# Two blocks' scatters at a time, directly ahead of norm1: a change to the order of GpSimd's queue in the first attention

## The chip, the cores and the metric

The kernel runs on one core of one Trainium2 chip. The metric is the time of one execution on the device in microseconds (us), lower is better. Engines: TensorE (PE, with its weight loads PEld), VectorE (DVE), ScalarE (ACT), GpSimd (POOL) and SyncE (SP), each with its own queue of instructions.

## What is computed

Two layers on x of 32 blocks of 128 tokens with 256 features. Each layer adds an attention and then a mixture of experts, both on a layer-normalised x:

```python
x = x + L0_xattn(layernorm(x), ctx, itok, mask, ...)   # 16 heads, masked by equal layer indices
x = x + L0_ffn(layernorm(x), router, w1, w2, scale)    # 8 experts, top 2, silu
x = x + L1_xattn(layernorm(x), ctx, ...)               # both directions, gated
x = x + L1_ffn(layernorm(x), ...)                      # 8 experts, top 2, capacity 640
```

In L0_ffn each token goes to its two best experts. The kernel therefore makes, for each block of 128 tokens, two lists of 128 slots (k = 0 and 1), and writes the tokens' numbers at those slots into a table in DRAM.

## The kernel before, in words

The program has four stages one after the other: first attention (a_*), first experts (b_*), second attention (c_*), second experts (d_*). In each stage every engine has a function that writes its whole queue out by hand. Engines meet by semaphores only.

**First attention.** A software pipeline over blocks b. In iteration b of its loop (b from 0 to NB + 4 = 36) GpSimd does work for different blocks: norm2(b - 2), the last three small steps of the second layer norm's factors (lines 449 to 453, behind VectorE's statistics of line 922); mask(b + 1) (line 465); add_bias(b - 1) (line 471); norm1(b + 4), the same for the first layer norm (lines 437 to 441, behind line 906). ScalarE reads norm1's result in L531 and norm2's in L625. VectorE works out the slots of a group of blocks at once (slots_out, lines 1012 to 1026); the groups are six of four blocks (0 to 23) and four of two (24 to 31). Its slots_out of a group whose last block is l runs in VectorE's iteration l + 4 and raises slot_ready.

**Scatters.** GpSimd writes each block's 128 token numbers to DRAM with two indirect DMAs (line 479, k = 0 and 1), 64 in all. The table `turn` says in which iteration a block's turn comes: for groups of four in iteration first + 8 + j, one block each iteration; for blocks 24 to 31, two blocks each in iterations 33, 34, 35 and 36. In an iteration with a turn the k = 0 scatters stand between mask and add_bias, and the k = 1 scatters behind norm1.

**The seam to the first experts.** After its loop GpSimd waits until all scatters have landed (line 511). Then b_pool waits for t_ready, which VectorE raises with etab (line 1230) at the end of `tables`, which in turn follows the last slots_out. Then come load_ids (line 1163: row numbers from the scattered table) and gather (line 1171: the rows). ScalarE and VectorE split the rows in two parts (lines 1275 and 1253), SyncE transposes them by DMA, and TensorE starts the first expert block (line 1324).

Of the kernel before, what the change touches and what calls it, by code (L numbers as in the profile page):

```python
# [23 lines left out]
NB = 32  # L24
# [33 lines left out]
def build(nc, a, out):  # L58
    with ExitStack() as ctx:
# [22 lines left out]
        def sem(name):  # L82

            s = nc.alloc_semaphore(name=name)
            owned.append(s)
            return s
# [4 lines left out]
        def dram_ids(name, n, k):  # L91
            return nc.dram_tensor("dram_" + name, (n, k), I32, kind="Internal").ap()
# [6 lines left out]
        ids = [dram_ids("ids0", SPARE0 + P, 1), dram_ids("ids1", SPARE1, 2)]  # L99
# [45 lines left out]
        tokens = sb("tokens", [P, NB], I32)  # L145
# [26 lines left out]
        def due(v):  # L172

            return not isinstance(v, int) or v > 0
# [32 lines left out]
        scat = [sem(f"a_scat{i}") for i in range(4)]  # L207
# [3 lines left out]
        def first_attention():  # L211
# [3 lines left out]
            def sa(name, shape, dt=F32):  # L215
                return work(name, shape, dt)
# [42 lines left out]
            RG = 4  # L259
# [5 lines left out]
            gslot, gsidx = sa("gslot", [P, RG * 2]), sa("gsidx", [P, 4, RG * 2], U32)  # L265
# [28 lines left out]
            cnt_done, cnt_read, slot_steps, slot_ready = (psem(n) for n in ("cnt_done", "cnt_read", "slot_steps", "slot_ready"))  # L294
# [3 lines left out]
            GROUPS = [(b, RG) for b in range(0, NB - 2 * RG, RG)] + [(b, 2) for b in range(NB - 2 * RG, NB, 2)]  # L298
            group_of = {}
# [4 lines left out]
            def inside(b):  # L304
                return 0 <= b < NB

            def last_of(b):

                if not inside(b):
                    return None  # L310
                g, j, n = group_of[b]
                return g if j == n - 1 else None
# [88 lines left out]
            def a_pool(pool):  # L401
                bound = pool.to_reg(SPARE0 - 1)
# [28 lines left out]
                def norm1(b):  # L431
                    if inside(b):
                        p = b % 2
                        pool.wait_ge(n1_stat, b + 1)
                        if due(b - 1):
                            pool.wait_ge(xn_ready, b - 1)
                        pool.tensor_scalar(rstd1[:, p, 0:1], mv1[:, p, 1:2], EPS, None, ALU.add).then_inc(n1_rstd, 1)
                        pool.wait_ge(n1_rstd, b * 3 + 1)
                        pool.tensor_tensor(rstd1[:, p, 0:1], rstd1[:, p, 0:1], minus_half[:, :], ALU.pow).then_inc(n1_rstd, 1)
                        pool.wait_ge(n1_rstd, b * 3 + 2)  # L440
                        pool.tensor_scalar(rstd1[:, p, 1:2], mv1[:, p, 0:1], rstd1[:, p, 0:1], -1.0, ALU.mult, ALU.mult).then_inc(n1_rstd, 1)
# [25 lines left out]
                def add_bias(b):  # L467

                    if inside(b):
                        pool.wait_ge(xn_ready, b + 1)  # L470
                        pool.tensor_tensor(x8[:, b % 8, :], x8[:, b % 8, :], bob[:, :], ALU.add).then_inc(res_ready, 1)

                def scatter(b, k):

                    g, j, n = group_of[b]
                    if j == 0 and k == 0:
                        pool.wait_ge(slot_ready, g + 1)
                    at = 2 * j + k
                    pool.indirect_dma_start(ids[0], bass.IndirectOffsetOnAxis(ap=gsidx[:, g % 4, at:at + 1], axis=0),  # L479
                                            tokens[:, b:b + 1], None, bounds_check=bound, oob_is_err=False).then_inc(scat[g % 4], 16)  # L480


                turn = {}
                for g, (first, n) in enumerate(GROUPS):
                    for j in range(n):
                        b = first + j
                        turn.setdefault(first + n + 4 + j if n == RG else NB + 4 - (NB - 1 - b) // 2, []).append(b)

                norm1(0)
                mask(0)  # L490
# [6 lines left out]
                norm1(3)  # L497
                pool.wait_ge(bo_ready, 1)
                pool.wait_ge(s_const, 64)
                for b in range(NB + 5):  # L500
                    norm2(b - 2)
                    if b > 0:
                        mask(b + 1)
                    for c in turn.get(b, ()):
                        scatter(c, 0)
                    add_bias(b - 1)
                    norm1(b + 4)
                    for c in turn.get(b, ()):
                        scatter(c, 1)
                for p in range(4):  # L510
                    pool.wait_ge(scat[p], scattered(len(GROUPS) - 1, p))

# [598 lines left out]

            a_sems = owned[kept:]
            return a_sync, a_pool, a_act, a_pe, a_dve, clear


# [1387 lines left out]
```

## Time and profile before

| | |
|---|---|
| median of three runs | 1536.67 us (1535.08 to 1537.13) |
| the profiled execution | 1535.08 us, span 1533.3 us |
| busy: TensorE, weight loads | 1355.9 us (88%), 1100.8 us (72%) |
| busy: VectorE, ScalarE, GpSimd | 848.4, 815.3, 669.3 us |
| first attention | up to about 391 us |
| first expert matmul | 429.28 us |
| the 64 scatters of line 479 | 68.2 us busy |

The profile is of one execution. The span runs from the first to the last recorded instruction, and the execution's own time is 1.8 us longer. Busy time is that of an engine's instructions; semaphore waits and the issue of DMAs by SyncE aren't counted in it. "Issue" in the chain of waits is time in which the engine waited for nothing that the profile shows.

### The profile page before, as it was taken

How to read it: one execution, taken by the hardware profiler on the slowest of the kernel's cores; microseconds unless marked ns; L12 is line 12 of the kernel's file. 1: busy time of each engine (PE TensorE's matmuls, PEld its weight loads, DVE VectorE, ACT ScalarE, POOL GpSimd, SP SyncE). 2: the span in 40 equal slices, each digit the busy share in tenths (PEclk: the TensorE clock that was granted, in tenths of full speed). 3: DMA queues.
4: the chain of work that ended last, by engine and by line, in shares of the span. 5: the costliest groups of instructions: out<-in, count | busy, mean ns of one | idle time of the engine just before them, and what ended most of it. 6: DMA issues, size and time to landing. Idle time of an engine off the chain costs nothing.

```text
span 1533.3 us, 37441 instructions
## 1 busy us (share of the span) xinstructions
PE 1355.9 (88%) x12922; PEld 1100.8 (72%) x12922; DVE 848.4 (55%) x2343; ACT 815.3 (53%) x1904; POOL 669.3 (44%) x935
## 2 busy tenths in 40 slices
PE   5999999997159999999997899999992899999996
PEld 4787777775126666667665788888881799999995
DVE  4787787876512323232222577777763566666663
ACT  3787777775035555554553555555551445545452
POOL 3234545453563333332301456666656344444422
PEclk8999999998579999999999999999995999999998
DMA  4333434341049999988886222232213343443331
GB/s 113 111 113 98 120 94 106 104 90 53 11 87 183 187 204 184 179 170 145 166 170 138 65 84 83 84 84 83 84 54 74 94 131 109 130 127 108 121 114 51
DMA packets 280856, 172.76 MB, mean 113 GB/s; under 512 B 212990, under 2 KB 259424, under 8 KB 280676
## 3 DMA queue, kind: packets, MB, share of 16 engines
q1 hardware_dynamic: 257940, 134.65, 38.3%
q0 software_dynamic: 18608, 32.14, 7.7%
q10 hardware_dynamic: 4128, 3.57, 0.8%
q8 instruction: 112, 1.84, 0.6%
q14 instruction: 68, 0.56, 0.2%
HBM read 93.40 MB, written 31.80 MB: 82 GB/s over the span
## 4 chain that ended last, share of the span: by engine, by line
PE 77%; DVE 5%; issue 4%; ACT 4%; DMA 3%; POOL 3%; another core or an unknown queue 1%; SPq 1%; ACTq 0%; DVEq 0%; POOLq 0%
PE psum L2267 14%; PE psum L1337 11%; PE psum L1324 11%; PE psum L2280 7%; PE psum L1804 3%; PE psum L1885 3%; PE psum L1810 3%; PE psum L797 2%; PE psum L726 2%; PE psum L700 2%; PE psum L739 2%; PE psum L814 2%; PE psum L800 2%; PE psum L1875 2%; PE psum L778 2%
## 5 line engine op out<-in xcount | busy, mean ns | idle before, releaser
L1260 DVE SCALAR_TENSOR_TENSOR b_h<-b_hid,b_h 128x1024 f16<-128x1024 f32 x71 | 87.0, 1226 | 283.8 <-ACT b_h L1289 278.7
L2267 PE MATMUL psum<-d_xT,d_w 128*128 128x256 f16 (+1 forms) x2304 | 230.0, 256 | 3.8 <-DVE d_xT L2356 2.9
L1324 PE MATMUL psum<-arena,b_xT 128*128 x852 | 200.0, 386 | 32.6 <-DMA b_xT<-b_x 32.1
L2267 PEld LDWEIGHTS psum<-d_xT,d_w 128*128 128x128 f16 x2304 | 199.6, 98 | 24.5 <-issue 2.5
L1337 PE MATMUL psum<-arena,b_hT 128*128 x1704 | 200.9, 274 | 14.1 <-issue 7.4
L1337 PEld LDWEIGHTS psum<-arena,b_hT 128*128 128x128 f16 x1704 | 166.4, 98 | 52.7 <-issue 19.4
L1324 PEld LDWEIGHTS psum<-arena,b_xT 128*128 128x128 f16 x852 | 84.6, 99 | 123.6 <-issue 40.7
L1284 ACT ACTIVATE b_hid<-psum 128x512 f32<-128x512 f32 x142 | 84.6, 597 | 137.1 <-PE psum L1324 83.9
L1171 POOL DMA_INDIRECT b_xg<-dram_normed,b_gi x71 | 67.3, 948 | 206.8 <-DVE b_x L1253 195.1
L2321 ACT ACTIVATE d_sg<-psum 128x256 f32<-128x256 f32 (+1 forms) x192 | 65.9, 348 | 143.9 <-PE psum L2267 135.9
L2366 DVE SCALAR_TENSOR_TENSOR d_hf<-psum,d_sg 128x256 f32<-128x256 f32 (+1 forms) x192 | 71.2, 379 | 103.7 <-ACT d_sg L2321 86.8
L2280 PE MATMUL psum<-d_w,d_h 128*128 128x256 f16 x960 | 115.5, 273 | 0.7 <-DVE d_h L2371 0.7
L594 ACT ACTIVATE pT<-psum,amc 128x512 f32<-128x512 f32 x128 | 77.5, 688 | 47.1 <-PE psum L726 47.1
L2280 PEld LDWEIGHTS psum<-d_w,d_h 128*128 128x128 f16 x960 | 90.9, 98 | 11.0 <-DVE d_h L2371 1.0
L1621 POOL DMA_INDIRECT c_yg<-dram_expert_rows,c_gi x64 | 64.8, 1012 | 70.2 <-DMA dram_expert_rows<-b_ys 55.2
L941 DVE TENSOR_REDUCE mx<-psum 128x4 f32<-128x512 f32 x128 | 79.5, 683 | 25.6 <-PE psum L700 25.4
L2229 POOL DMA_INDIRECT out<-d_rowsum,d_gi x40 | 42.1, 1053 | 92.4 <-DVE d_rowsum L2381 85.1
L2224 POOL DMA_INDIRECT d_rowsum<-out,d_gi x40 | 43.2, 1079 | 87.5 <-PE psum L2267 63.1
L1163 POOL DMA_INDIRECT b_gi<-dram_ids,ypos x71 | 67.4, 950 | 27.2 <-issue 27.2
L1289 ACT ACTIVATE b_h<-b_hid 128x1024 f16<-128x1024 f32 x71 | 75.0, 1057 | 4.6 <-DMA b_hT<-b_h 2.5
L1656 POOL DMA_INDIRECT dram_ids<-c_gsidw,c_gsidx x64 | 67.6, 1057 | 19.4 <-issue 19.4
L479 POOL DMA_INDIRECT dram_ids<-tokens,gsidx x64 | 68.2, 1066 | 12.9 <-issue 12.9
(319 smaller groups left out, 2933.0 us busy)
## 6 DMA issues: line engine op xcount, KB each, us to landing
d_wst<-in_L_w SPq DMA_DIRECT2D x64, 384.0 KB
stage<-in_L_w SPq DMA_DIRECT2D x32, 512.0 KB
dram_expert_rows<-b_ys SPq DMA_DIRECT2D x71, 128.0 KB
ctxT<-in_ctxT SPq DMA_DIRECT2D x64, 128.0 KB
dram_normed<-xn SPq DMA_DIRECT2D x64, 128.0 KB
x<-in_x SPq DMA_DIRECT2D x32, 128.0 KB, 4.9
dram_x<-xnew SPq DMA_DIRECT2D x32, 128.0 KB
c_x<-dram_x SPq DMA_DIRECT2D x32, 128.0 KB
```

The lines of the kernel that those rows point to most:

```text
L479: pool.indirect_dma_start(ids[0], bass.IndirectOffsetOnAxis(ap=gsidx[:, g % 4, at:at + 1], axis=0), tokens[:, b:b + 1], None, bounds_check ...
L594: act.activation(pT[:, r, :, :].rearrange("p j q -> p (j q)"), psum[:, SB + r, :], ACT.Exp, bias=amc[:, b:b + 1]).then_inc(exp_done[r], 1)
L941: i = dve.tensor_reduce(mx[:, r, :], psum[:, SB + r, :].rearrange("p (j k) -> p j k", j=HB), AX.X, ALU.max)
L1260: dve.scalar_tensor_tensor(out=h16[:, p, 1, :], in0=hid[:, p, :], scalar=H_SCALE, in1=h16[:, p, 0, :], op0=ALU.mult, op1=ALU.subtract).the ...
L1284: act.activation(hid[:, p, half * 512:(half + 1) * 512], psum[:, 1 + 2 * p + half, :], ACT.Silu, scale=1.0 / (X_SCALE * W_SCALE)).then_inc ...
L1289: act.activation(h16[:, p, 0, :], hid[:, p, :], ACT.Copy, scale=H_SCALE).then_inc(hi_done, 1)
L1324: i = pe.matmul(psum[:, 1 + 2 * p + half, :], xT[:, j % NT, px, c, :], weights(e, c, pw, half * 512, 512), start=(n == 0), stop=(n == len( ...
L1337: i = pe.matmul(psum[:, 6 + p, 0:D], hT[:, p, ph_, c, :], weights(e, 2 + c // 4, pw, (c % 4) * D, D), start=(n == 0), stop=(n == len(terms ...
L1656: pool.indirect_dma_start(ids[1], bass.IndirectOffsetOnAxis(ap=gsidx[:, g % 3, at:at + 1], axis=0), gsidw[:, g % 3, at, :], None, bounds_c ...
L2267: i = pe.matmul(psum[:, q, m * n:(m + 1) * n], w16[:, fc % RING, pw, col:col + P], xT[:, p, px, c, at:at + n], start=(k == 0), stop=(k == ...
L2280: i = pe.matmul(psum[:, NQ + k, 0:D], h16[:, fc % 2, ph_, k * P:(k + 1) * P], w16[:, fc % RING, pw, 2 * DC * P:UW], start=(fc == 0 and t = ...
L2366: dve.scalar_tensor_tensor(out=hf[:, fc % 2, at:at + n], in0=psum[:, q, n:2 * n], scalar=H_SCALE / (X_SCALE * W_SCALE), in1=sg[:, fc % 2, ...
```

## The change

The table `turn` is gone. scatter(b) now issues both indirect DMAs of a block, one behind the other, and the loop calls it in one place only, between add_bias and norm1. When the group of block b - 5 ends with that block, the group's first two blocks are scattered in iteration b; when the group of block b - 6 ends with that block, its third and fourth are. For a group whose last block is l these are iterations l + 5 and l + 6. Blocks 24 to 31 thus have their turns in iterations 30, 32, 34 and 36. Nothing else is changed.

```diff
--- before.py
+++ after.py
@@ -470,21 +470,15 @@
                         pool.wait_ge(xn_ready, b + 1)
                         pool.tensor_tensor(x8[:, b % 8, :], x8[:, b % 8, :], bob[:, :], ALU.add).then_inc(res_ready, 1)
 
-                def scatter(b, k):
-
-                    g, j, n = group_of[b]
-                    if j == 0 and k == 0:
-                        pool.wait_ge(slot_ready, g + 1)
-                    at = 2 * j + k
-                    pool.indirect_dma_start(ids[0], bass.IndirectOffsetOnAxis(ap=gsidx[:, g % 4, at:at + 1], axis=0),
-                                            tokens[:, b:b + 1], None, bounds_check=bound, oob_is_err=False).then_inc(scat[g % 4], 16)
-
-
-                turn = {}
-                for g, (first, n) in enumerate(GROUPS):
-                    for j in range(n):
-                        b = first + j
-                        turn.setdefault(first + n + 4 + j if n == RG else NB + 4 - (NB - 1 - b) // 2, []).append(b)
+                def scatter(b):
+                    if inside(b):
+                        g, j, n = group_of[b]
+                        if j == 0:
+                            pool.wait_ge(slot_ready, g + 1)
+                        for k in range(2):
+                            at = 2 * j + k
+                            pool.indirect_dma_start(ids[0], bass.IndirectOffsetOnAxis(ap=gsidx[:, g % 4, at:at + 1], axis=0),
+                                                    tokens[:, b:b + 1], None, bounds_check=bound, oob_is_err=False).then_inc(scat[g % 4], 16)
 
                 norm1(0)
                 mask(0)
@@ -497,16 +491,18 @@
                 norm1(3)
                 pool.wait_ge(bo_ready, 1)
                 pool.wait_ge(s_const, 64)
+
                 for b in range(NB + 5):
                     norm2(b - 2)
                     if b > 0:
                         mask(b + 1)
-                    for c in turn.get(b, ()):
-                        scatter(c, 0)
                     add_bias(b - 1)
+                    for last, at in ((b - 5, 0), (b - 6, 2)):
+                        if last_of(last) is not None:
+                            first, n = GROUPS[last_of(last)]
+                            for j in range(at, min(at + 2, n)):
+                                scatter(first + j)
                     norm1(b + 4)
-                    for c in turn.get(b, ()):
-                        scatter(c, 1)
                 for p in range(4):
                     pool.wait_ge(scat[p], scattered(len(GROUPS) - 1, p))
```

## Rows read from the trace of the kernel before

**Rows 1.** Windows: us; each engine's busy (x instructions); PEclk, DMA share, GB/s.
```profile
286.35:330.14 43.79, 41.60 (x597) 33.40 (x593) 34.56 (x105) 33.77 (x84) 22.98 (x41) 1.00 0.40 103
...
391.37:418.54 27.17, 1.98 (x10) 1.40 (x10) 16.64 (x71) 1.49 (x5) 16.57 (x18) 0.50 0.03 5
...
480.00:840.00 360.00, 351.68 (x2427) 239.17 (x2425) 100.97 (x132) 188.97 (x322) 104.76 (x114) 1.00 0.92 173
```

**Rows 2.** Waits from 154 to 330: us in total, times, longest us.
```profile
POOL rstd L437 <- DVE mv L906: 68.7, 16, 6.0
```

**Rows 3.** The chain of waits in the seam: start us, us, what.
```profile
406.24 8.14 DMA dram_ids<-tokens,gsidx
414.38 4.16 issue
```

**Rows 4.** GpSimd's timeline in the seam: start us, us, engine, line, operation, [idle before].
```profile
391.11 0.26 POOL L453 TENSOR_SCALAR rstd<-mv,rstd 128x1 f32<-128x1 f32 x1
391.54 1.07 POOL L479 DMA_INDIRECT dram_ids<-tokens,gsidx  x1 [0.16 <-issue]
392.92 0.98 POOL L479 DMA_INDIRECT dram_ids<-tokens,gsidx  x1 [0.30 <-issue]
...
411.69 0.97 POOL L479 DMA_INDIRECT dram_ids<-tokens,gsidx  x1 [0.30 <-issue]
418.54 1.00 POOL L1163 DMA_INDIRECT b_gi<-dram_ids,ypos  x1 [5.87 <-issue]
```

**Rows 5.** VectorE's timeline in the seam.
```profile
392.38 0.21 DVE L1026 CAST gsidx<-gslot 128x4 uint32<-128x4 f32 x1
...
398.26 0.16 DVE L1026 CAST gsidx<-gslot 128x4 uint32<-128x4 f32 x1
...
407.28 0.20 DVE L1230 CAST etab<-b_tables 128x71 int32<-128x71 f32 x1
```

**Rows 6.** The chain of waits at the second attention's end.
```profile
1174.46 2.07 DMA dram_ids<-c_gsidw,c_gsidx
```

**Rows 7.** Timeline of GpSimd, ScalarE and VectorE, one iteration of the steady part.
```profile
286.35 0.24 POOL L437 TENSOR_SCALAR rstd<-mv 128x1 f32<-128x1 f32 x1 [5.63 <-DVE mv L906]
...
287.34 0.27 POOL L441 TENSOR_SCALAR rstd<-mv,rstd 128x1 f32<-128x1 f32 x1
287.77 1.08 POOL L479 DMA_INDIRECT dram_ids<-tokens,gsidx  x1 [0.16 <-issue]
...
288.93 0.23 POOL L449 TENSOR_SCALAR rstd<-mv 128x1 f32<-128x1 f32 x1
...
290.14 0.74 POOL L465 TENSOR_SCALAR other<-tokr,tokc 128x128 f32<-128x128 f32 x1
291.06 1.08 POOL L479 DMA_INDIRECT dram_ids<-tokens,gsidx  x1 [0.18 <-issue]
292.18 0.73 POOL L471 TENSOR_TENSOR x<-x,bob 128x256 f32<-128x256 f32 x1
...
295.86 0.62 ACT L531 ACTIVATE xn<-x,rstd 128x256 f32<-128x256 f32 x1
296.24 0.18 DVE L906 BATCH_NORM_AGGREGATE mv<-st 128x2 f32<-128x6 f32 x1
296.35 0.62 ACT L625 ACTIVATE xn<-xnew,rstd 128x256 f32<-128x256 f32 x1
```

**Rows 8.** GpSimd's timeline in the drain, iterations 32 and 33.
```profile
380.90 0.23 POOL L449 TENSOR_SCALAR rstd<-mv 128x1 f32<-128x1 f32 x1 [7.16 <-DVE mv L922]
...
382.10 0.72 POOL L471 TENSOR_TENSOR x<-x,bob 128x256 f32<-128x256 f32 x1
390.14 0.22 POOL L449 TENSOR_SCALAR rstd<-mv 128x1 f32<-128x1 f32 x1 [7.32 <-DVE mv L922]
```

**Rows 9.** Timeline of TensorE and ScalarE at the start of the experts.
```profile
429.28 10.22 PE L1324 MATMUL psum<-arena,b_xT 128*128 x36 [32.07 <-DMA b_xT<-b_x]
...
444.11 0.60 ACT L1284 ACTIVATE b_hid<-psum 128x512 f32<-128x512 f32 x1 [7.75 <-remote]
```

**Rows 10.** Line 479 alone: duration ns min/median/max, first and last start us.
```profile
L479 POOL DMA_INDIRECT dram_ids<-tokens,gsidx x64: 971/1078/1525, 114.7 to 411.7; - x64
```

## The prediction

> **What bounds the kernel now.** I read the table of windows first. While blocks flow steadily, four blocks take 43.79 us and TensorE is busy for 41.60 of them at the full granted clock (1.00, 2.4 GHz); GpSimd is busy for 22.98 [rows 1]. So TensorE with its short hand-overs sets the pace there, and GpSimd has spare time. The list of waits of that stretch says the same from the other side: GpSimd waits for VectorE (68.7 us in 16 waits, 4.3 us each, before norm1), and among the waits of the other engines none names GpSimd as the one waited for [rows 2]. From 391.37 to 418.54 the picture turns over: 27.17 us in which TensorE is busy for 1.98, VectorE for 16.64 and GpSimd for 16.57 [rows 1]. This is the seam between the first attention and the first experts.
>
> In the seam the chain of waits runs through GpSimd alone: scatter after scatter of L479, then a transfer of 8.14 us and 4.16 us charged to nothing, until the first row-number load of the experts at 418.54 [rows 3]. GpSimd's timeline shows the whole row of them: 16 of the 64 scatters start from 391.54 to 411.69, all of them after the last norm2 [rows 4]. They are the scatters of blocks 24 to 31, which the old table of turns puts in iterations 33 to 36, while norm2 of block 31 is in iteration 33. The reader is to see that these 20 us are a backlog and not work waiting for its input. VectorE hands over the slots of the last but one pair at 392.38 + 0.21 = 392.59 and of the last pair at 398.26 + 0.16 = 398.42, and the last table that the experts' first load needs (etab) at 407.28 + 0.20 = 407.48 [rows 5]. GpSimd is behind all three.
>
> **The change, part by part.** (1) *What moves out of the seam.* With the new rule, blocks 24 and 25 scatter in iteration 30, 26 and 27 in iteration 32, 28 and 29 in 34, 30 and 31 in 36. Of the 16 scatters in the seam, 8 leave it. The number of scatters stays 64, and the wait for slot_ready stays one for each group.
>
> (2) *The new seam.* It starts as before, at 391.37, with the end of norm2 of block 31 (391.11 + 0.26). Blocks 28 and 29 wait for slots until 392.59. The first scatter of the old run starts 0.16 us after the engine is free, the second starts 392.92 − 391.54 = 1.38 us later, and from the second to the last are 14 steps in 18.77 us, with two long ones among them; I take the common step, 0.97 us of work and 0.30 us of gap, 1.27 [rows 4]. So the four start at 392.75, 394.13, 395.40 and 396.67 and GpSimd is free at 397.9. The last four wait for slots until 398.42 and start at 398.58, 399.96, 401.23 and 402.50. The last scatter thus starts 411.69 − 402.50 = 9.19 us earlier.
>
> (3) *From the last scatter to the experts' first load.* GpSimd waits until every scatter has landed. Before, the load starts 418.54 − 411.69 = 6.85 us after the last scatter's start [rows 4]. How much of this is landing and how much depends on the backlog isn't shown. From below: in the same place of the second attention the chain gives a scatter's landing as 2.07 us [rows 6]; then the last one would be down at 404.57, the tables at 407.48 would decide, and with 0.30 of gap the load starts at 407.78, a gain of 10.76. From above: the chain gives 8.14 us for the fifth from the end [rows 3]; with the same gap the load starts at 402.50 + 8.14 + 0.30 = 410.94, a gain of 7.60. I take 6.85, since it is measured on the same scatter with the same three ahead of it at the same spacing: the load starts at 409.35 and the gain is 9.19. The tables (407.48) are then 1.9 us early.
>
> The Trainium skill ("DMA: Bandwidth & Descriptors", Anatomy of one DMA — SWDGE (gpsimd) path) gives such a transfer a fixed cost of about 2.0 us beside its bytes, most of it the wait for the write's receipt. By it the tables would decide and the estimate would be a gain of 10.8. The row of the second attention agrees with it (2.07), the row of this seam doesn't (6.85, if all of it is landing).
>
> (4) *The steady part: 12 bursts of four in place of pairs, the last two of them in the drain.* For groups of four, iterations 0 and 1 modulo 4 get four scatters each after add_bias and the other two get none. In the old iteration, norm1 runs from 286.35 to 287.61, a scatter lies ahead of norm2 (287.77) and another behind mask (291.06), and add_bias ends at 292.91. Without the two, norm2, mask and add_bias close up: 1.24 us are saved ahead of norm2 and 1.26 behind mask, so add_bias ends at 290.41. The burst starts 0.17 later and takes 1.08 + 3 × 1.27 = 4.89, until 295.47. The next norm1 can't start before its statistics, 296.24 + 0.18 = 296.42 [rows 7]. The cover is GpSimd's wait for VectorE, and 0.95 us of it are left. If that cover is gone, norm1 is late, and what is late next is the normalisation on ScalarE, L531: it starts at 295.86 for a norm1 that ended at 287.61, 8.25 us of further slack [rows 7]. Price: nothing. norm2 gets earlier by 1.2 us, and its reader on ScalarE (L625) starts at 296.35 anyway [rows 7], so there is no gain either.
>
> (5) *The drain.* Here iterations wait for norm2's statistics and bursts lie in those waits. The tightest is the last, blocks 26 and 27 in iteration 32: norm2 of block 30 starts at 380.90 and add_bias ends at 382.10 + 0.72 = 382.82; the burst ends at 382.82 + 0.17 + 4.89 = 387.88, and the norm2 of block 31 starts at 390.14 [rows 8]. 2.26 us are left. Without that cover each us would be lost one for one, as ScalarE, the logits and the last slots hang on this norm2. Price: nothing.
>
> (6) *Behind the seam.* The first expert matmul starts at 429.28 after 32.07 us without TensorE work [rows 9]; it moves with the load, 10.74 us behind it. From 480 to 840 TensorE is busy for 351.68 of 360.00 us [rows 1], so the experts are bound by work of fixed length and the gain is carried to the end. What isn't sure is the start of the experts: ScalarE waits 7.75 us for something that the trace doesn't name, until 444.11 [rows 9]. I take it as unchanged, with 3 us either way for the range. The granted clock is 0.50 (1.2 GHz) all through the seam, after TensorE had nearly stopped [rows 1], and still when the experts start; I expect the same.
>
> **The sum.** −9.19 (seam) + 0 (steady) + 0 (drain) = −9.2. The profiled execution has a span of 1533.3 and took 1535.08, so it would become 1524.1 and 1525.9. The median of the three runs is 1536.67, 1.6 above that execution; from it I get 1527.5 us, 0.60% less. A measurement of this kernel can tell about 0.2% (3.1 us) from no change.
>
> **The rivals.** (a) *The landing is short and the tables decide.* For it: 2.07 us in the second attention [rows 6]. Against it: the scatters there hold another record and may drop more rows, and here 6.85 us passed. Time: 1536.67 − 10.76 = 1525.9. Chance 0.15. (b) *Given back at the experts' start*, by the unnamed waits or a clock that rises later: half of the gain is lost. For it: the 7.75 us wait; against it: all that feeds it moves along. Time: 1532.1, chance 0.10. (c) *No change*: the experts' first load is held by something else that stands at 418. For it: 4.16 us of the chain before that load are charged to nothing [rows 3]. Against it: 6.85 us is short for another cause to hide behind. Time: 1536.7, chance 0.05. (d) *Slower: bursts of four stall GpSimd in the steady part.* Place: between add_bias and norm1, iterations 8 to 29. It decides once a burst exceeds 4.89 + 0.95 + 8.25 = 14.09 us, 3.5 us for a scatter; from there each us costs 12. With 4.0 us a scatter it is (16.0 − 14.09) × 12 = 23 us, less the 9 of the seam: 1550.5. Against it: the longest of 64 scatters takes 1.525 us, the 16 in a row included [rows 10]. Chance 0.03.
>
> **How the numbers follow.** The forecast has 0.67 and gives 1527.5; its own range is 7.60 to 10.76 of gain and 3 us of the start, 1523 to 1532. (a) lies inside, (b) at its edge. I give 1524.0 to 1532.5, which leaves out (c), (d) and little of the rest. Faster by over 0.2% is the forecast, (a) and most of (b): 0.90. Within 0.2%: (c) and the rest of (b): 0.07. Slower: 0.03.
>
> **What the changed profile would show.** Right: 8 scatters between norm2 of block 31 and the experts' first load, in two runs of four with a gap of about 0.7 us before the second; the load at 409.4 (407.8 would mean the tables, 410.9 a longer landing); the first expert matmul at 420.1; TensorE's idle time before it near 23 us. The four-block period stays at 43.8 us and GpSimd's idle time before norm1 falls to about 1 us after bursts and grows after the others. Wrong: norm1 or norm2 of the steady part named as a wait of ScalarE; norm2 of block 31 later than 390.2; a scatter of over 2 us; or a gap between the load and the first matmul of more than 11 us.

## The result, and the profile of the changed kernel

The change makes the kernel slower.

| | before | changed |
|---|---|---|
| median of four runs, same chip | 1535.88 us (1533.14 to 1537.13) | 1556.24 us (1552.75 to 1562.42) |
| ratio | | 1.014, 95% interval 1.0104 to 1.0175 |
| profiled execution, its span | 1535.08 us, 1533.3 us | 1566.01 us, 1564.2 us |

Forecast were 1527.5 us and a range of 1524.0 to 1532.5. The rows below explain the profiled pair, which lies 30.9 us of span apart, half again the 20 us between the medians; the profiled execution of the changed kernel is the slowest of its five.

I cut both spans at the same events: VectorE's first-norm statistics of block 12 and of block 31, its second-norm statistics of block 31, the end of GpSimd's norm2 of block 31, and the experts' first row-number load. First the table of windows of the kernel before (columns as in rows 1), steady part and drain:

```profile
120.30:329.90 209.60, 198.22 (x2805) 159.42 (x2807) 165.68 (x495) 161.51 (x394) 109.21 (x190) 1.00 0.41 105
329.90:389.90 60.00, 47.73 (x599) 35.55 (x596) 40.91 (x137) 31.80 (x78) 21.59 (x35) 0.85 0.23 53
```

The same of the changed kernel; the last two lines are the seam, which answers to the second of [rows 1], and all that follows:

```profile
119.90:364.40 244.50, 214.50 (x2806) 170.20 (x2808) 164.36 (x495) 162.75 (x396) 107.10 (x189) 0.93 0.44 90
364.40:427.50 63.10, 46.47 (x597) 34.62 (x594) 40.03 (x136) 31.95 (x78) 28.23 (x42) 0.88 0.29 50
429.06:448.58 19.52, 1.98 (x10) 1.40 (x10) 15.82 (x65) 1.29 (x4) 8.21 (x8) 0.50 0.03 7
448.60:1564.20 1115.60, 1006.44 (x8212) 821.40 (x8212) 546.53 (x1419) 542.85 (x1244) 483.09 (x588) 0.96 0.51 120
```

The seam did shrink, from 27.17 to 19.52 us, by 7.65. The steady part grew by 34.9 us and the drain by 3.1. Behind the load nothing changed (1115.6 against 1533.3 − 418.54 = 1114.8). GpSimd is busy for 2.1 us *less* in the longer steady part, and TensorE does the same 2806 matmuls. Its idle time grew from 209.60 − 198.22 = 11.4 to 30.0 us, and the matmuls themselves took 16.3 us longer at a granted clock of 0.93 instead of 1.00. So what happened is that TensorE stood still for 18.6 us, and its clock fell with it.

The list of waits of the steady part says at whose door. First the kernel before (us in total, times, longest):

```profile
POOL rstd L437 <- DVE mv L906: 80.6, 19, 6.0
ACT pT L594 <- PE psum L726: 27.1, 19, 1.4
```

And the changed kernel:

```profile
POOL rstd L437 <- DVE mv L902: 67.5, 11, 9.2
DVE xnew L912 <- PE psum L810: 43.9, 14, 4.9
POOL rstd L449 <- DVE mv L918: 35.9, 13, 4.4
ACT pT L590 <- remote: 31.5, 8, 5.0
ACT pT L590 <- PE psum L722: 17.8, 11, 2.7
ACT oT L599 <- remote: 9.3, 1, 9.3
```

GpSimd waits more than before (norm2, L449, waits for VectorE for 35.9 us), and nobody waits for GpSimd. New are waits of ScalarE for "remote", a releaser that the profile can't name: a semaphore update is recorded at the time at which the wait ended, but no instruction that makes this update had ended shortly before. The timeline around one row of four scatters shows what they are; changed kernel, TensorE, GpSimd, ScalarE and VectorE:

```profile
162.08 1.11 POOL L480 DMA_INDIRECT dram_ids<-tokens,gsidx  x1 [0.17 <-issue]
...
163.05 1.08 PE L722 MATMUL psum<-qeo,kT 32*128 32x256 f32 x13
...
163.49 0.97 POOL L480 DMA_INDIRECT dram_ids<-tokens,gsidx  x1 [0.30 <-issue]
...
164.77 0.97 POOL L480 DMA_INDIRECT dram_ids<-tokens,gsidx  x1 [0.30 <-issue]
...
166.04 1.48 POOL L480 DMA_INDIRECT dram_ids<-tokens,gsidx  x1 [0.30 <-issue]
...
167.04 0.18 DVE L902 BATCH_NORM_AGGREGATE mv<-st 128x2 f32<-128x6 f32 x1
167.14 1.97 ACT L590 ACTIVATE pT<-psum,amc 128x512 f32<-128x512 f32 x3 [4.40 <-remote]
167.60 0.24 POOL L437 TENSOR_SCALAR rstd<-mv 128x1 f32<-128x1 f32 x1
```

The exponential of L590 reads the scores that the matmuls of L722 leave, and waits for nothing else that is late. These matmuls end at 163.05 + 1.08 = 164.13. ScalarE starts at 167.14, 3.01 us later, inside the last scatter. In the iteration of [rows 7], the kernel before has the same hand-over with no scatter beside it, and it takes 0.04 us: the matmuls end at 293.27 and the exponential starts at 293.31. Its timeline:

```profile
292.19 1.08 PE L726 MATMUL psum<-qeo,kT 32*128 32x256 f32 x13
293.31 2.42 ACT L594 ACTIVATE pT<-psum,amc 128x512 f32<-128x512 f32 x4 [1.43 <-PE psum L726]
```

GpSimd, meanwhile, does what was forecast: the row takes 5.44 us, and norm1 (L437) starts 0.08 us after it, 0.38 us behind its statistics. The row costs GpSimd nothing. It is TensorE's signal that arrives late while the row is being issued.

That the signal is late, and not ScalarE in reading it, stands in the trace's record of semaphore updates. The update that this exponential waits for is recorded at 167.11, 2.98 us behind the matmuls' end, and ScalarE starts 0.02 us behind the update. (In the kernel before the update stands at 293.28, 0.01 us behind the matmuls' end.) The ends of matmuls are modelled, but TensorE's next matmuls, L793, start at 164.06, so a later true end doesn't explain 3 us. The same record for all waits of ScalarE in the steady part that a signal of TensorE ended:

| what GpSimd was at when the matmul ended | update behind the matmul's end, median | waits |
|---|---|---|
| no indirect DMA, kernel before | 0.01 us | 47 |
| no indirect DMA, changed kernel | 0.07 us | 32 |
| a single scatter, kernel before | 1.01 us | 4 |
| a row of four, changed kernel | 1.81 us, at most 6.74 | 14 |

The signals of ScalarE, VectorE and GpSimd that ended a wait came within 0.02 us in the steady part of every profile, those raised during a row included. The latest signal outlasts its row: the last scatter ends at 328.59 + 0.97 = 329.56, the matmuls ended at 324.95, and ScalarE's copy starts at 331.87. A single scatter holds a signal too, for less time. The kernel before shows this in the iteration of [rows 7], where a scatter starts at 287.77: the matmuls of L739 end at 288.33, the last of their updates stands at 289.25, and the copy starts at 289.43. First these two lines, then those of the changed kernel:

```profile
287.25 1.08 PE L739 MATMUL psum<-pT,v 128*32 128x128 f32 x32
...
289.43 0.60 ACT L603 ACTIVATE oT<-psum 128x512 f32<-128x512 f32 x1 [1.28 <-PE psum L739]
```

```profile
323.83 1.12 PE L735 MATMUL psum<-pT,v 128*32 128x128 f32 x28
...
331.87 0.60 ACT L599 ACTIVATE oT<-psum 128x512 f32<-128x512 f32 x1 [9.31 <-remote]
```

VectorE's statistics show the price: the four iterations that end at 167.04 (above) and in the last three of these lines take 9.38, 14.11, 13.32 and 11.92 us, where the same four of the kernel before take 10.21, 10.13, 11.27 and 12.47.

```profile
157.66 0.18 DVE L902 BATCH_NORM_AGGREGATE mv<-st 128x2 f32<-128x6 f32 x1
...
181.15 0.18 DVE L902 BATCH_NORM_AGGREGATE mv<-st 128x2 f32<-128x6 f32 x1
...
194.47 0.18 DVE L902 BATCH_NORM_AGGREGATE mv<-st 128x2 f32<-128x6 f32 x1
...
206.39 0.18 DVE L902 BATCH_NORM_AGGREGATE mv<-st 128x2 f32<-128x6 f32 x1
```

Nine whole rows lie in the steady window, so one costs 34.9 / 9 = 3.9 us on average, the slower clock included.

The seam of the changed kernel, GpSimd and TensorE, beside [rows 4] and [rows 9]:

```profile
428.79 0.27 POOL L453 TENSOR_SCALAR rstd<-mv,rstd 128x1 f32<-128x1 f32 x1
430.49 1.07 POOL L480 DMA_INDIRECT dram_ids<-tokens,gsidx  x1 [1.44 <-DVE gsidx L1022]
...
436.36 0.97 POOL L480 DMA_INDIRECT dram_ids<-tokens,gsidx  x1 [0.97 <-DVE gsidx L1022]
...
440.19 1.32 POOL L480 DMA_INDIRECT dram_ids<-tokens,gsidx  x1 [0.31 <-issue]
...
448.58 0.99 POOL L1159 DMA_INDIRECT b_gi<-dram_ids,ypos  x1 [7.07 <-DMA dram_ids<-tokens,gsidx]
...
459.42 1.89 PE L1320 MATMUL psum<-arena,b_xT 128*128 x4 [24.55 <-DMA b_xT<-b_x]
```

From the end of norm2 (429.06) to the last scatter are 11.13 us, as forecast (402.50 − 391.37 = 11.13). From there to the load are 8.39 us and not 6.85.

### The profile page after: what moved, and what is told of

It is laid out like the page before. It is cut to its first block, busy times and chain, and to the rows that moved or that the text cites. A ratio compares the mean times of both kernels' runs of the same rounds, so it can differ in the third digit from the quotient of the medians.

```text
span 1564.2 us, 37441 instructions
## 1 busy us (share of the span) xinstructions
PE 1369.4 (88%) x12922; PEld 1108.9 (71%) x12922; DVE 846.5 (54%) x2343; ACT 816.8 (52%) x1904; POOL 669.9 (43%) x935
## 4 chain that ended last, share of the span: by engine, by line
PE 72%; DVE 6%; issue 6%; ACT 5%; another core or an unknown queue 4%; DMA 3%; POOL 2%; ACTq 0%; SPq 0%; DVEq 0%; POOLq 0%
PE psum L2263 14%; PE psum L1333 11%; PE psum L1320 11%; PE psum L2276 7%; PE psum L1800 3%; PE psum L1881 3%; PE psum L1806 3%; PE psum L810 2%; PE psum L696 2%; PE psum L735 2%; PE psum L1871 2%; DMA b_hT<-b_h 2%; PE psum L793 1%; PE psum L722 1%
## 5 line engine op out<-in xcount | busy, mean ns | idle before, releaser
L1333 PE MATMUL psum<-arena,b_hT 128*128 x1704 | 200.3, 274 | 14.3 <-DMA b_hT<-b_h 9.2
L1333 PEld LDWEIGHTS psum<-arena,b_hT 128*128 128x128 f16 x1704 | 165.9, 98 | 53.3 <-issue 20.8
L590 ACT ACTIVATE pT<-psum,amc 128x512 f32<-128x512 f32 x128 | 78.2, 688 | 76.6 <-remote 41.3
```

The source lines that it names most:

```text
L590: act.activation(pT[:, r, :, :].rearrange("p j q -> p (j q)"), psum[:, SB + r, :], ACT.Exp, bias=amc[:, b:b + 1]).then_inc(exp_done[r], 1)
L1333: i = pe.matmul(psum[:, 6 + p, 0:D], hT[:, p, ph_, c, :], weights(e, 2 + c // 4, pw, (c % 4) * D, D), start=(n == 0), stop=(n == len(terms ...
```

## The experiments

The kernels were timed in batches, each on one chip and with the kernel before in it, and each ratio is to the kernel before of the same batch. In two of the batches (that of e5_row_behind_norm1, e9 and e11, and that of e18) the kernel before had 1512.5 and 1512.4 us, in all others 1533.8 to 1542.4; I call the two the quick batches, for the difference matters below. "Steady part" and "seam" are the stretches of a profile between the events named above, the seam here from VectorE's last second-norm statistics to the load: 209.5 and 28.7 us before, 244.4 and 21.1 us changed.

### The change in halves: the tail alone, and one block an iteration

e1_old_steady_new_tail is the kernel before with new turns for the last eight blocks only:

```diff
-  turn.setdefault(first + n + 4 + j if n == RG else NB + 4 - (NB - 1 - b) // 2, []).append(b)
+  turn.setdefault(first + n + 4 + j if n == RG else first + 6, []).append(b)
```

> The kernel before, with the new turns for blocks 24 to 31 alone (iterations 30, 32, 34, 36; each turn still two k = 0 scatters ahead of add_bias and two k = 1 behind norm1). Theory H (held signals: while GpSimd issues scatters back to back, TensorE's semaphore signals arrive late, and only long rows of them hurt): the steady part stays at 43.8 us for four blocks, the seam is 8 to 9 us shorter, 1527 to 1530 us. Theory L (late GpSimd: what the bursts cost is norm1, norm2 or mask coming late): the same, as no burst is in the steady part. Theory P (place: scatters between add_bias and norm1 meet a hand-over of TensorE, however many they are): the same. If it is not faster than before, the seam's gain was not real.

e2_pairs_ahead_of_norm1 has the changed kernel's place, but one block an iteration for the groups of four, so that two scatters stand next to each other:

```diff
 add_bias(b - 1)
-for last, at in ((b - 5, 0), (b - 6, 2)): ...
+for g, (first, n) in enumerate(GROUPS):
+    if n == RG and 0 <= b - first - 8 < RG:
+        scatter(b - 8)
+    if n == 2 and b == first + 6:
+        scatter(first)
+        scatter(first + 1)
 norm1(b + 4)
```

> The changed kernel, but in groups of four one block in each iteration (two scatters back to back between add_bias and norm1); blocks 24 to 31 as in the changed kernel. H: a row of two holds TensorE's signals for about 2 us, mostly without harm: 1527 to 1540 us. L: GpSimd has 2.5 us less to do in an iteration with a burst, no loss: 1527 to 1530. P: twice as many iterations meet the place: as slow as the changed kernel or slower, 1550 or more.

Measured: e1 1530.31 us, 0.9945 (0.9921 to 0.9969), steady part 209.4, seam 20.6. e2 1529.45 us, 0.994 (0.9917 to 0.9964), steady part 207.7, seam 20.6. What follows: the gain of the seam is real and comes through to the end. The place ahead of norm1 and pairs cost nothing. The loss needs the four.

### Is it GpSimd's time, or that of the transfers?

e4_busy_without_dma is the kernel before, with GpSimd kept busy for some 5 us where the row of four would be, by additions:

```diff
 add_bias(b - 1)
+if 8 <= b < 30 and b % 4 < 2:
+    for i in range(6):                       # ... each waits for the one before
+        pool.tensor_tensor(spare[:, :], bob[:, :], bob[:, :], ALU.add).then_inc(spare_steps, 1)
 norm1(b + 4)
```

> The kernel before with 6 additions of 128x256 (about 0.75 us each, 5 us in all, on a tile of their own) added between add_bias and norm1 in iterations 0 and 1 modulo 4, from 8 to 29; the scatters stay where they were. So GpSimd is as busy as in the burst, and longer in all, without DMA. H: the steady part unchanged, 1534 to 1539 us. L: norm1 is as late or later than in the changed kernel: 1556 or more. P says nothing.

e8_changed_small_stage is the changed kernel with the loads of the experts' weights (L352, 512 KB for a block) cut to a sixteenth from block 2 on, e8b_before_small_stage the same cut of the kernel before. Both leave out 15/16 of these weights.

```diff
-  sp.dma_start(stage[:, b % 2, :], chunk(a["L0_w"], b)).then_inc(stage_ld[b % 2], 16)
+  n = F if b < 2 else F // 16
+  sp.dma_start(stage[:, b % 2, 0:n], chunk(a["L0_w"], b)[:, 0:n]).then_inc(stage_ld[b % 2], 16)
```

> The changed kernel with the weights' stage loads from block 2 on cut to a sixteenth (32 KB in place of 512 KB), so the expert weights beyond are wrong; about half of the traffic on the DMA engines in the first attention is gone. If the hold needs DMA engines busy with other transfers (theory HC, contention), the rows of four cost little: the four-block period is near 44 us and the time 1525 to 1535. If rows of scatters hold the signals by themselves: a period near 49 us and 1550 or more.

> The kernel before with the same cut of the stage loads: the base for the run above. All theories: TensorE sets the pace, period 43 to 44 us, 1530 to 1537 us.

e6_gather_bursts is the kernel before plus a row of four small indirect *loads* (4 bytes in each of 128 partitions) in the place of the row; e11_direct_dma_rows the same with four direct loads of the same size, issued by GpSimd too.

```diff
+# ... if 8 <= b < 30 and b % 4 < 2, and when the last such row has landed:
+for i in range(4):
+    pool.indirect_dma_start(got[:, i, :], None, a["tokT"].rearrange("b p a -> (b p) a"),      # e6
+                            bass.IndirectOffsetOnAxis(ap=tokens[:, i:i + 1], axis=0)).then_inc(got_ld, 16)
+    pool.dma_start(got[:, i, :], a["tokT"][i:i + 1].rearrange("b p a -> (b p) a")).then_inc(got_ld, 16)   # e11
```

> The kernel before with four indirect loads back to back (128 elements of 4 bytes each from DRAM to SBUF, read by nobody) added between add_bias and norm1 in iterations 0 and 1 modulo 4, 8 to 29: the same issue work for GpSimd in the same place as the changed kernel's rows of four, but loads in place of scatters. If a row of any indirect DMAs holds TensorE's signals (theory HI, issue): 1550 to 1565 us. If it takes the small writes to DRAM (theory HW, writes): 1535 to 1540 us.

> As the run with rows of four indirect loads, but the four are direct loads of the same shape (128 elements of 4 bytes) issued by GpSimd. If any DMA issued by GpSimd in a row holds the signals: as slow as those indirect loads, 1% or more above the kernel before. If it takes the indirect form: within 0.3% of before.

Measured: e4 1533.49 us, 0.9969 (0.9942 to 0.9996), steady part 209.4. e8 1563.99, 1.0157 (1.0116 to 1.0198), steady part 233.3; e8b 1542.31, 1.0007 (0.9978 to 1.0035), 209.4. e6 1568.72, 1.0169 (1.0115 to 1.0222), 229.4. e11 1508.96, 0.9972 (0.9949 to 0.9995), 199.3. The windows of the steady parts of e4, e8 and e11, one line of each kernel's table:

```profile
121.10:330.50 209.40, 199.91 (x2797) 160.15 (x2795) 170.94 (x494) 160.42 (x391) 156.01 (x246) 0.98 0.45 105
```

```profile
120.30:353.50 233.20, 204.28 (x2805) 162.60 (x2807) 163.41 (x493) 162.79 (x396) 105.35 (x189) 0.98 0.29 55
```

```profile
121.10:320.40 199.30, 195.36 (x2801) 157.86 (x2799) 168.47 (x493) 160.86 (x393) 130.25 (x226) 1.00 0.45 111
```

In e4 GpSimd is busy for 156 us instead of 109 and the stretch has its old length: GpSimd has the time for the row, as forecast. In e8 the DMA engines are busy for 29% and move 55 GB/s instead of 90, and the loss stays: it is no contest with the loads of these weights. e6 shows that no scatter is needed, nor writes to DRAM; indirect loads do it. In e11 a row of direct DMAs, which issues in about half the time (574 ns each instead of 1041), does no harm. This was a quick batch, where rows of four scatters harm less too; but e5 of the same batch (below) has them and 1518.81 us, a new tail included, against the 1508.96 of e11. In the quick batches TensorE's signals are hardly held even beside indirect DMAs (below), so what rows of direct DMAs do in an ordinary batch isn't shown.

### How long must the row be?

e9_rows_of_three spreads the eight scatters of a group of four over three iterations (3, 3, 2):

```diff
+at = b - first - n - 4
+if 0 <= at < 3:
+    for i in range(3 * at if n == RG else 4 * at, min(3 * at + 3 if n == RG else 4 * at + 4, 2 * n)):
+        scatter(first + i // 2, i % 2)
```

> The changed kernel, in groups of four three scatters back to back in each of iterations 0 and 1 modulo 4 and two in iteration 2, in place of four, four and none. If the hold grows with each scatter of a row: between rows of two and rows of four, 1533 to 1545 us. If it needs a fourth: 1527 to 1532.

e7_row_spaced is the changed kernel with two additions of GpSimd between any two scatters of a row, and e13_two_and_two has a single addition, between the second and the third:

```diff
 def space_out():
+    for i in range(2):                       # e13: range(1); ... each waits for the one before
+        pool.tensor_tensor(spare[:, :], bob[:, :], bob[:, :], ALU.add).then_inc(spare_steps, 1)
 ...
-                            for k in range(2):
+    if apart and (j % 2, k) != (0, 0):       # e13: == (1, 0)
+        space_out()
```

> The changed kernel, but in groups of four the four scatters of a row have two additions of 128x256 (0.75 us each) between them, so they start some 2.8 us apart in place of 1.3; iterations and place are the same, GpSimd is busy for 4.5 us more. HI and HW both say that the spaces let the signals through: 1527 to 1535 us. Theory P (place): as slow as the changed kernel, 1550 or more.

> The changed kernel with one addition of GpSimd between the second and the third scatter of each row. Theory that an unbroken row of more than two holds the signals: the loss is nearly gone, ratio 0.994 to 1.000. Rival that four scatters within some 7 us suffice, broken or not: 1.008 or more.

Measured: e9 1514.24 us, 1.0006 (0.9986 to 1.0026), steady part 213.3. e7 1541.47, 1.0 (0.9972 to 1.0027), 216.7. e13 1539.01, 1.0008 (0.9978 to 1.0039), 213.4; the changed kernel on e13's chip (after_again, below) has 1563.72. One addition of 0.7 us thus takes back 25 of the 1563.7 us without moving a scatter out of its iteration. Timeline of e13, TensorE, GpSimd and ScalarE:

```profile
158.85 1.08 PE L735 MATMUL psum<-qeo,kT 32*128 32x256 f32 x13
159.29 0.98 POOL L493 DMA_INDIRECT dram_ids<-tokens,gsidx  x1 [0.30 <-issue]
160.26 0.65 POOL L481 TENSOR_TENSOR spare<-bob 128x256 f32<-128x256 f32 x1
160.77 2.42 ACT L603 ACTIVATE pT<-psum,amc 128x512 f32<-128x512 f32 x4 [2.22 <-PE psum L735]
161.08 0.99 POOL L493 DMA_INDIRECT dram_ids<-tokens,gsidx  x1 [0.17 <-issue]
162.38 1.33 POOL L493 DMA_INDIRECT dram_ids<-tokens,gsidx  x1 [0.31 <-issue]
```

The matmuls end at 159.93 and ScalarE starts at 160.77, 0.84 us later, during the addition. With the row unbroken it waited 3.01 us. Neither e7 nor e13 reaches the 0.994 of e1 and e2, so a part of the loss is left. In e7 two waits of VectorE (3.9 us together) still have no releaser, and some of the loss has another cause, since its additions make the mask late; its waits:

```profile
DVE nother L938 <- POOL other L467: 14.2, 8, 3.2
```

What three in a row cost isn't settled. e9 ran in a quick batch, and there e18 (below), with no row at all in the steady part, has the same ratio within the uncertainty.

### The place, and the chip

The changed kernel again (after_again), with the row behind norm1 (e5_row_behind_norm1, and e5_again on the chip of after_again) and with the row behind norm2 (e12_row_behind_norm2):

```diff
 norm2(b - 2)
+# e12: the row here
 mask(b + 1)
 add_bias(b - 1)
-# the changed kernel: the row here
 norm1(b + 4)
+# e5: the row here
```

> The changed kernel with the rows of four behind norm1 in place of ahead of it. HI (a row of indirect DMAs issued back to back holds TensorE's signals, wherever it stands): 1545 to 1570 us. P (place between add_bias and norm1 is what hurts): 1527 to 1535.

> The changed kernel once more, so that the next three have it on the same chip. Theory (a row of four indirect DMAs holds TensorE's signals back) and rival (the loss belongs to the chip it was measured on) differ here: theory 1.012 to 1.016 of the kernel before, four-block steady period near 50 us; rival below 1.008.

> The row of four behind norm1, again, now beside the changed kernel on one chip. If the place in the iteration matters, this stays near 1.005 while the changed kernel shows 1.014. If only the chip made the earlier run look better, both show the same ratio within 0.3%.

> The row of four behind norm2, ahead of the mask: a third place. If what TensorE issues during the row decides the price, the ratio lies between 1.003 and 1.012, different from both others of this batch; if the place is indifferent, it is the changed kernel's 1.014.

Measured in one batch: after_again 1563.72 us, 1.0172 (1.0126 to 1.0218), e5_again 1572.02, 1.0233 (1.0188 to 1.0278), e12 1566.43, 1.0215 (1.0152 to 1.0278). In a quick batch, e5_row_behind_norm1: 1518.81, 1.0052 (1.002 to 1.0083), outside both expected ranges; so are the ratios of e12 and of e5_again. No place is safe, which fells what I had read from the first e5. Only the signal that is caught changes. In e5_again it is that of the last matmuls into the output (L735), and ScalarE's copy L599 waits (VectorE has eight waits for "remote" there too, 19.0 us in all); TensorE, GpSimd and ScalarE:

```profile
176.11 0.46 PE L735 MATMUL psum<-pT,v 128*32 128x128 f32 x4 [0.26 <-issue]
176.60 0.97 POOL L480 DMA_INDIRECT dram_ids<-tokens,gsidx  x1 [0.30 <-issue]
178.81 0.60 ACT L599 ACTIVATE oT<-psum 128x512 f32<-128x512 f32 x1 [4.77 <-remote]
```

And the price isn't fixed: ten executions of the first e5 lie between 1508.03 and 1527.29 us, and the profiled one was the fastest. Its steady part has 203.6 us, that of e5_again 243.6. The semaphore records show what differs. In the ordinary batches TensorE's signals to ScalarE come, in the median of a profile, 1.53 to 3.02 us late beside a row of four (seven profiles), 0.54 and 0.56 beside two (e2, e13) and 0.51 to 1.01 beside a single scatter. In the quick batches it is 0.12 us beside the rows of four of e5, 0.01 beside the rows of three of e9, and 0.12 and 0.01 beside the single scatters of e11 and e18. The chip's number doesn't decide: e18 ran on the one of after_again (9), where the kernel before had 1538.49 us.

### The same scatters in the same iterations, not next to each other

e3_four_apart, and e16_four_apart_again on the chip of e15_changed_beside_apart, which is the changed kernel once more. An iteration issues the same four scatters as in the changed kernel:

```diff
 norm2(b - 2)
+for c in todo[0:1]: scatter(*c)
 mask(b + 1)
+for c in todo[1:2]: scatter(*c)
 add_bias(b - 1)
-for last, at in ((b - 5, 0), (b - 6, 2)): ...   # all four
+for c in todo[2:3]: scatter(*c)
 norm1(b + 4)
+for c in todo[3:4]: scatter(*c)
```

> The changed kernel's turns (four scatters in iterations 0 and 1 modulo 4), but the four stand apart: behind norm2, behind mask, behind add_bias and behind norm1. H: no row of scatters, so no long hold: 1527 to 1537 us. L: GpSimd is as late in these iterations as in the changed kernel, norm2 and mask later still: 1550 or more. P: one scatter in place of four at the place: about a quarter of the loss, 1532 to 1537.

> The changed kernel, beside the spread one on one chip. Theory: 1.012 to 1.018 of the kernel before where the chip is like the former ones; if the price of a row belongs to the chip as well, it may be as small as 1.005.

> Same turns as the changed kernel, each scatter behind another step of the iteration, so none stands next to another. Theory: no signal is held, the seam's 8 us are kept: 0.993 to 0.996 whatever the chip, and 1.2 to 2.4% below the changed kernel on the same chip. Rival (four scatters in an iteration cost by their number): the steady part is longer by more than 5 us and the ratio is over 1.000.

Measured: e3 1529.01 us, 0.9937 (0.9909 to 0.9966). On one chip, e15 1560.03, 1.0172 (1.013 to 1.0215), and e16 1526.7, 0.9951 (0.9927 to 0.9974): 33 us apart. Steady part and waits of e16:

```profile
122.90:327.40 204.50, 197.06 (x2801) 158.07 (x2803) 168.75 (x494) 160.65 (x393) 112.46 (x189) 1.00 0.52 108
```

```profile
ACT pT L600 <- PE psum L732: 29.6, 19, 1.9
```

TensorE idles for 204.5 − 197.1 = 7.4 us and keeps the full clock, all 19 waits of the exponential have their releaser in TensorE, none for "remote". Like e1 and e2, this version beats both kernels.

### Does the kernel before pay the same price at the experts' start?

There GpSimd issues indirect loads back to back from 418.54 to 446.30, and ScalarE has two waits of 7.75 [rows 9] and 6.44 us for "remote". Kernel before, TensorE, GpSimd and ScalarE:

```profile
442.56 0.94 POOL L1171 DMA_INDIRECT b_xg<-dram_normed,b_gi  x1 [0.30 <-issue]
443.81 0.94 POOL L1163 DMA_INDIRECT b_gi<-dram_ids,ypos  x1 [0.30 <-issue]
...
444.06 2.75 PE L1337 MATMUL psum<-arena,b_hT 128*128 x12 [4.56 <-issue]
...
451.14 0.60 ACT L1284 ACTIVATE b_hid<-psum 128x512 f32<-128x512 f32 x1 [6.44 <-remote]
```

The semaphore records say what these waits are. Matmuls of L1324 end at 435.62, 436.92, 438.21 and 439.51, and the next four updates of their semaphore are recorded at 444.08, 451.12, 451.22 and 451.29. Taken in order, the signals are 8.5 to 14.2 us late, and each wait ends 0.02 to 0.03 us behind an update. TensorE, meanwhile, is at later matmuls (L1337) from 444.06 on. So signals are held in the kernel before too, beside a longer row; what this costs in time isn't shown.

e18_experts_row_broken is e3 with one addition of GpSimd after each pair of these loads, for blocks 2 to 12:

```diff
 load_ids(j + 2)
 gather(j)
+if 2 <= j < 13:
+    pool.wait_ge(spare_steps, spared)
+    pool.tensor_tensor(spare[:, :], spare[:, :], spare[:, :], ALU.add).then_inc(spare_steps, 1)
```

> The spread version, and in addition the row of some 22 indirect loads that GpSimd issues at the start of the first experts broken by one addition after each pair, for blocks 2 to 12. In the kernel before ScalarE waits there twice for a releaser that isn't named, 7.75 and 6.44 us, while that row is issued beside a busy TensorE. Theory (the row holds TensorE's signals there too): these two waits shrink below 2 us, and 5 to 10 us are gained beside those of the spread version: 0.987 to 0.991 of the kernel before. Rival (the waits have another cause): they stay, and the ratio is that of the spread version, 0.9937 to 0.9951, or above it since GpSimd has eleven additions more.

Measured, in a quick batch: 1511.67 us, 0.9993 (0.997 to 1.0016), steady part 205.8, seam 20.8. The ratio isn't the theory's 0.987 to 0.991. The two waits are gone. But they are gone as well in the profiles of e5_row_behind_norm1, e9 and e11, whose experts' start is the old one, while every profile of the other batches has them (13.6 to 14.3 us together, 8.0 in e6). So the experiment does not tell whether the additions removed them. Nor does it show the gain of the spread version in a quick batch: with a drain of 60.3 and a seam of 20.8 it is 3.3 us shorter there than e11 (53.5 and 31.0), and its steady part is 6.5 us longer (205.8 against 199.3).

## Why the prediction was wrong

**The step that failed is (4)**, the steady part, "Price: nothing". It measured +34.9 us in the profiled pair. The step counted right what it counted: the row (forecast 4.89 us from first start to last end, 5.44 in the iteration shown) fits into GpSimd's wait, norm1 is fed, and e4 shows that 5 us of other work cost nothing. What it left out is that issuing the row is not GpSimd's business alone. A signal that TensorE raises meanwhile arrives up to several us late, TensorE then runs dry behind ScalarE's exponential, and its clock falls too. Shown by runs are: the late hand-over (in the timelines and the semaphore records), that indirect loads do it too (e6), that it needs them next to each other (e16 against e15, e13 against after_again, in one batch each), and that neither the place, nor GpSimd's load, nor the weights' loads explain it. What in the chip holds the signal was not found, nor what makes a batch quick.

**Rival (d)** has the right sign and the right place and was given 0.03, but its mechanism is wrong. It let GpSimd be the late one, from 3.5 us a scatter on. The longest scatter of the changed kernel takes 1.73 us and the common one 0.97. The three other rivals didn't occur. In the steady part of the kernel before no scatter stands next to another [rows 7], and the 16 in a row stand in the seam, where TensorE is idle [rows 1]. A row beside a busy TensorE was in the trace all the same, at the experts' start, together with a wait that names no releaser [rows 9]. So was the signal held by a single scatter: in the iteration of [rows 7] ScalarE's copy starts 1.10 us behind its matmuls' end, of which the last update's delay is 0.92. I read that wait as a risk of step (6) and not as a sign of what a row does. An estimate from such a row, with the 6 to 8 us that ScalarE waited there, would have been several us each, times twelve.

**Steps (1) to (3)**, the seam: the mechanism is right. The eight scatters are gone from it and the last one starts 9.19 us earlier against norm2, to the hundredth as forecast (11.13 us behind it instead of 20.32). The hundredth is luck: single starts are up to 0.10 us off and cancel, and other profiles with this tail have 10.53 to 11.23. The term that was off is the 6.85 us from the last scatter to the load: 8.39 here, so the gain is 7.65, at the lower bound (7.60). It varies between profiles with the same tail: in e16 the load comes 6.76 us behind the last scatter. The other profiles with the old tail (e4, e6, e8b, e11) have a seam of 30.6 to 31.0 us, and all with the new tail 19.5 to 21.1 (the profiled kernel before has 28.7), so some 10 us of seam are the more usual gain, of which a longer drain takes a part. The wait ends on the landing (7.07 us for the DMA's signal), the tables don't decide. The 2.0 us that the Trainium skill gives ("DMA: Bandwidth & Descriptors", Anatomy of one DMA — SWDGE (gpsimd) path) are not what these scatters take to land.

**Step (5)**, the drain, priced at nothing: +3.1 us. e2, which issues the last eight blocks' scatters in the same rows of four but has pairs in iterations 28 and 29, has a drain of 58.7 us, where the changed kernel has 63.1, 65.6 and 65.0 in three profiles. That points to the two rows in which TensorE is still busy; it was not tested by itself. **Step (6)** held: the first expert matmul stands 10.84 us behind the load (before 10.74), and the rest has its length.

Without long rows in the steady part, about the forecast's 0.60% less is measured in the ordinary batches: e1, e2, e3 and e16 have its seam and 0.9945, 0.994, 0.9937 and 0.9951. In a quick batch e18, with the same spread, has 0.9993.

## What to carry to other kernels

When a change puts instructions next to each other that stood apart, look in the trace for such a row beside the engines that it will now run beside; a row that was harmless beside an idle TensorE tells nothing. Spread GpSimd's indirect DMAs between its other steps wherever TensorE hands work over in short cycles; two together cost nothing that could be measured here, and even one addition between two pairs took back most of the loss. In a profile, compare the end of the producing matmul with the start of its reader, and take waits for "remote" in a kernel on one core as a reason to look for late signals (on the path, "another core or an unknown queue" has 1% before and 4% after).

## What the runs showed of the hardware

- While GpSimd issues four indirect DMAs back to back (1.27 us apart), a signal of TensorE reaches ScalarE us after the matmul's end (3.01 us and at most 6.9 in the changed kernel, 2.24 in the iteration shown of e5_again), against 0.04 us without. Beside a single scatter it is about 1 us (1.01 in the kernel before). Signals of the other engines aren't held (within 0.02 us in every profile).
- Beside the experts' longer row of indirect loads TensorE's signals come 8.5 to 14.2 us late in the kernel before.
- The price depends on the length of the unbroken row: with two 0.994, with four 1.014 to 1.0233 and in a quick batch 1.0052; four with one addition in the middle 1.0008.
- Batches differ: the kernel before had 1512 us in two and 1534 to 1542 in the others. ScalarE's waits of 14 us for "remote" at the experts' start stand in the profiles of the latter alone, and e5 cost 0.5% in the one kind and 2.3% in the other, with executions from 1508 to 1527 us in the one. In the profiles of the quick batches TensorE's signals are hardly held (medians of 0.12 us and less).
- Idle TensorE can cost twice: in the profiled changed kernel the granted clock of the steady part fell to 0.93, and the same matmuls took 214.5 us instead of 198.2. How much the clock adds varies: in e8 TensorE idled for 28.9 us, much as in the changed kernel (30.0), but the clock was 0.98 and the matmuls took 204.3.
